# Gated delta attention with experts: k weighted ahead of the scan, z laid out by tokens, a mask by select, no product by the identity, and new task orders

## The chip, the cores and the metric

The kernel runs on one core of a Trainium2 chip. The metric is the device time of one execution in microseconds, the median of several runs. The core has TensorE (matrix products), VectorE, ScalarE and GpSimd (elementwise work), SyncE (which only issues DMAs here), SBUF for tiles, and PSUM, into which TensorE writes and which GpSimd does not read in this kernel. Each engine works through its own list of instructions in order; the engines meet only through semaphores.

## The reference

A layer with modulated layer norm, gated delta rule attention, a second layer norm and a mixture of six small experts (two per sample), for 8 samples of 512 tokens with 256 features. The part that the change touches is the attention: 16 key heads of 128, each with 2 value heads of 128. Cut to what matters:

```python
q, k, v = silu(conv4(h @ W_qkv.T))          # causal convolution over time, 4 taps
z = h @ W_z.T
q, k = l2norm(q) * dk ** -0.5, l2norm(k)
g = cumsum(g, within a chunk)
decay = where(tril, exp(g[:, None] - g[None, :]), 0)
A = -where(strict_tril, (beta * k) @ k.T * decay, 0)
T = inverse(eye - A)
value_, k_cumdecay = T @ (beta * v), T @ (beta * k * exp(g))
for each chunk:
    v_new = value_ - k_cumdecay @ state
    out = (q * exp(g)) @ state + where(tril, q @ k.T * decay, 0) @ v_new
    state = state * exp(g_last) + (k * exp(g_last - g)).T @ v_new
core = out * rsqrt(mean(out * out) + 1e-6)
y = (norm_weight * core * silu(z)) @ W_out.T
```

## The kernel before

`build` writes three stages. `modulation_and_gates` makes the first layer norm and all gate values and leaves them in DRAM. `attention` runs 128 steps, one for each pair of sample and key head. `experts` does the second norm, the choice of experts and their products. The change is in `attention`, but for one constant.

A step is cut into some 60 small tasks per engine, and the orders are written out as lists: `PE_ORDER`, `ACT_ORDER`, `DVE_ORDER`, `POOL_ORDER` (lines 34 to 44). An entry such as `M2@3` means: task M, part 2, of the step that is 3 ahead of this round's number. `loop` (line 510) walks the list once per round, two rounds in the body of a hardware loop, so that up to five steps are in flight and every engine repeats one list with the period of a step. Nothing moves an entry at run time: if one waits, all behind it on that engine wait. `t.wait(engine, name, k, back=b)` waits for the k-th signal of `name` of the step b before; `wait_newest` waits for the latest earlier user of a PSUM bank.

A step takes 4 chunks of 128 tokens (`NC`) and 2 value heads (`HD`), so 8 units (`U`). Its tasks, with what they hand on:

- TensorE P0 to P11 (line 658): the projection; tiles 0 to 3 are k, q and two of v, tiles 4 and 5 are z, all with channels on the partitions. ScalarE C and VectorE T0 to T11 (line 1018, three per tile) make the convolution, ScalarE SK, SQ, SV the silu, ScalarE Z (line 891) the silu of z into `z_t`.
- TensorE KT, QT, VT (lines 668 to 707): transposes to tokens; ScalarE KN, QN squares and VectorE KN, QN sums; GpSimd PW (line 1199) a power 0.5; VectorE SM0 to SM3 and SN0 to SN2 small scalings (lines 1034 to 1060; SN0 makes `w_c`, the factors of the state's update).
- GpSimd GL (line 1194): `low = g_row + bound`, where the constant `bound` is 0 or -1e30; ScalarE GE (line 924): eight exponentials of it into `dec`, behind a table load, since exponential and silu lie in different tables. TensorE KK0, KK1 (line 690): products of k by k and q. VectorE GA0 to GA3 (line 1072): `ga`, A and the attention weights. GpSimd SL (line 1203) sets the diagonal of A.
- The inverse of a 128 by 128 triangle: VectorE AB0, AB1 (line 1078) copy its two halves of 64 into `a_bd`; TensorE L, M1 to M5, Y1 to Y5 (lines 713 to 725), VectorE y0 to y5, q1 to q5, X1 to X5 (lines 1085 to 1102) and XB1 to XB5 on ScalarE (upper half, line 936) and GpSimd (lower half, line 1225) invert them level by level in bf16; Q, p, Z, XD, YC, XC join them; D0, D1, VectorE F0, F1 (line 1118), GpSimd RL (line 1217), G0, G1, ScalarE v0, v1 (line 970) and W0, W1 refine the result. W (line 793) adds, in PSUM, the old inverse by a product with the identity, and three more products; ScalarE IV0, IV1 (line 966) copy the sum into `inv_t`.
- The scan over chunks: TensorE KS, VectorE RR, TensorE TR; then VectorE VW (line 1140) makes `vw`, v_new times `w_c`, and ScalarE VX copies v_new into `vx`; TensorE U (line 826) is the product of `k_tok` and `vw`, VectorE ST adds it to the state, which GpSimd SD has decayed; TensorE O the output, ScalarE OT a copy.
- The output: ScalarE OQ sums of squares, VectorE OS0, OS1 (lines 1156, 1159), GpSimd OP (lines 1244, 1247: a power -0.5 and a product) and ON (line 1253: the scaling of `o_tok`); TensorE ON transposes it, VectorE HT (line 1164) multiplies by the norm weight and `z_t`, TensorE OY0, OY1 (line 868) the product by W_out, VectorE YA0, YA1 add it up.

KT, QT, VT, KK, D, G, W, ON and OY share the two PSUM banks `p_out`. SyncE feeds each step's weights and gate rows one to four steps ahead.

## Time and profile before

| | |
|---|---|
| median of three runs (lowest, highest) | 4832.42 us (4830.36, 4836.11) |
| span of the profiled execution | 4831.3 us |
| busy share of the span: TensorE, VectorE, ScalarE, GpSimd | 97%, 91%, 72%, 57% |
| mean granted TensorE clock | 0.987 |
| DMA | 377 MB, 78 GB/s, 24.7% of the engines' time |

The profile holds one execution. An instruction's duration reaches from its start to its end, and on TensorE the ends are modelled; consecutive instructions overlap, so what a task takes of its engine is better read as the distance from its start to the next start. "Idle before" is time in which the engine stood still ahead of an instruction, with the one that ended the wait. A product of float32 tiles is recorded as two matmul instructions.

### The profile page before, as it was taken

What the parts mean: (1) busy time and instruction counts of PE and PEld (TensorE: products, weight loads), DVE (VectorE), ACT (ScalarE), POOL (GpSimd) and SP (SyncE); (2) the same over time, 40 slices, a digit from 0 to 9 for tenths busy, and PEclk for the clock granted to TensorE, in tenths of its full rate; (3) what the DMA queues carried; (4) which work ended last, traced back from release to release, by engine and by line L of the source; (5) the groups of instructions that cost most, each with busy time, mean ns of one, the idle gap of its engine ahead of it and who ended that gap; (6) DMA issues with size and microseconds to landing.
All of it is one profiled execution on the core that took longest, in us unless ns stands there. A gap on an engine that the chain in (4) does not pass through costs nothing. (4 is left out here: it accounts for less than half of the span.)

```text
span 4831.3 us, 132942 instructions
## 1 busy us (share of the span) xinstructions
PE 4671.0 (97%) x38533; PEld 3195.1 (66%) x38788; DVE 4411.5 (91%) x9152; ACT 3467.6 (72%) x8336; POOL 2743.0 (57%) x2329
## 2 busy tenths in 40 slices
PE   5899999999999999999999999999999999999978
PEld 3566666666666666666666666666666666666643
DVE  4899999999999999999999999999999999999953
ACT  3677777777777777777777777777777777777732
POOL 2456665656565665656566665656566665656520
PEclk7999999999999999999999999999999999999988
DMA  4222222222222222222222222222222222222122
GB/s 156 65 75 79 68 86 70 88 66 87 67 79 79 68 86 71 88 66 87 67 80 79 68 86 66 92 66 84 70 78 80 66 87 66 92 66 84 55 79 83
DMA packets 185165, 377.26 MB, mean 78 GB/s; under 512 B 86400, under 2 KB 95744, under 8 KB 184960
## 3 DMA queue, kind: packets, MB, share of 16 engines
q1 hardware_dynamic: 185088, 376.46, 24.7%
q14 instruction: 57, 0.47, 0.0%
q8 instruction: 20, 0.33, 0.0%
HBM read 360.13 MB, written 16.25 MB: 78 GB/s over the span
## 5 line engine op out<-in xcount | busy, mean ns | idle before, releaser
L658 PE MATMUL p_proj<-hid,w_in 128*128 128x512 f32 x3072 | 1626.7, 612 | 30.0 <-POOL ident_h L1185 28.9
L1018 DVE SCALAR_TENSOR_TENSOR conv<-p_proj,taps,conv 128x509 f32<-128x509 f32 (+2 forms) x1536 | 1134.8, 739 | 48.2 <-ACT conv L886 34.9
L1199 POOL TENSOR_TENSOR root<-sums,half_pow 128x8 f32<-128x8 f32 x128 | 210.8, 1647 | 862.9 <-DVE sums L1028 843.9
L1225 POOL TENSOR_SCALAR_AFFINE_SELECT x_bd<-x_t 128x512 bf16<-128x512 bf16 x640 | 422.6, 660 | 213.5 <-DVE x_t L1102 211.2
L658 PEld LDWEIGHTS p_proj<-hid,w_in 128*128 128x128 f32 x3072 | 497.3, 192 | 55.1 <-POOL ident_h L1185 29.1
L1093 DVE TENSOR_TENSOR y_h<-p_lev,y_h 128x512 bf16<-128x512 f32 x640 | 440.2, 688 | 74.4 <-PE p_lev L725 74.4
L868 PE MATMUL p_out<-h_t,w_out 128*128 128x512 f32 x1024 | 476.5, 608 | 2.2 <-DVE h_t L1164 1.1
L936 ACT ACTIVATE x_bd<-x_t 64x512 bf16<-64x512 bf16 x640 | 397.7, 621 | 96.3 <-DVE x_t L1102 96.2
L1102 DVE STREAM_TRANSPOSE x_t<-y_h 128x512 bf16<-128x512 bf16 x640 | 450.3, 704 | 4.5
L1072 DVE SCALAR_TENSOR_TENSOR ga<-p_out,neg_c,dec 128x256 f32<-128x256 f32 x1024 | 412.9, 477 | 35.4 <-ACT dec L924 34.8
L886 ACT ACTIVATE conv<-p_proj,taps 128x512 f32<-128x512 f32 x512 | 351.7, 687 | 121.9 <-PE p_proj L658 119.3
L1085 DVE TENSOR_TENSOR q_h<-p_lev,consts 128x512 bf16<-128x512 f32 x640 | 429.6, 671 | 3.8 <-PE p_lev L718 3.8
L979 ACT ACTIVATE vx<-p_b 128x256 f32<-128x256 f32 x512 | 197.9, 386 | 285.8 <-PE p_b L816 161.4
L1217 POOL TENSOR_TENSOR r_lo<-resid 128x1024 bf16<-128x1024 f32 x128 | 242.3, 1893 | 247.9 <-DVE resid L1118 247.9
L838 PE MATMUL p_b<-vx,ga 128*128 128x128 f32 x2048 | 375.1, 275 | 0.0
L868 PEld LDWEIGHTS p_out<-h_t,w_out 128*128 128x128 f32 x1024 | 184.6, 190 | 285.0 <-DVE ga L1072 147.9
L725 PEld LDWEIGHTS p_lev<-q_h,x_bd 128*128 128x128 bf16 x5120 | 216.5, 97 | 213.5 <-issue 101.5
L985 ACT ACTIVATE o_tok<-p_b 128x256 f32<-128x256 f32 x512 | 194.1, 379 | 199.5 <-PE p_b L838 196.4
L718 PEld LDWEIGHTS p_lev<-y_h,a_bd 128*128 128x128 bf16 x5120 | 222.7, 98 | 152.1 <-issue 84.2
L1232 POOL TENSOR_TENSOR q_dec<-kq,e_row 128x512 f32<-128x512 f32 x256 | 320.0, 1271 | 0.0
L924 ACT ACTIVATE dec<-low,g_neg 128x128 f32<-128x128 f32 x1024 | 313.3, 388 | 1.6
L1244 POOL TENSOR_TENSOR o_sc<-o_sc,neg_half 128x8 f32<-128x8 f32 x128 | 211.4, 1651 | 168.9 <-DVE o_sc L1159 168.9
(213 smaller groups left out, 12562.4 us busy)
## 6 DMA issues: line engine op xcount, KB each, us to landing
w_in<-in_w_in SPq DMA_DIRECT2D x128, 768.0 KB, 6.3
g_row<-rows_scratch SPq DMA_DIRECT2D x128, 512.0 KB, 3.2
hid<-h_scratch SPq DMA_DIRECT2D x128, 512.0 KB, 7.4
e_row<-exp_rows_scratch SPq DMA_DIRECT2D x128, 512.0 KB, 5.3
w_out<-in_w_out SPq DMA_DIRECT2D x128, 256.5 KB, 2.7
x<-in_x SPq DMA_DIRECT2D x8, 512.0 KB, 10.6
...
```

The lines of the kernel that those rows point to most:

```text
L658: last = pe.matmul(p_proj[tile % 2][:], w_in[p][:, kt, tile * P:(tile + 1) * P], hid[p][:, kt, :], start=(kt == 0), stop=(kt == KT - 1))
L838: last = pe.matmul(p_b[:, at], ga[p][:, n * HD + h, 1, :], vx[:, h, :], start=(n == 0), stop=True)
L868: last = pe.matmul(p_out[n][:], w_out[p][:, h * D + n * P:h * D + (n + 1) * P], h_t[:, :, h, :], start=(h == 0), stop=(h == HD - 1))
L886: act.activation(conv[:, n, :], p_proj[n % 2][:], ACT.Copy, scale=taps[p][:, n, PAD:PAD + 1])\
L936: act.activation(x_bd[0:HB, :, 0:HB], x_t[0:HB], ACT.Copy).then_inc(s["xbd"], 1)
L1018: dve.scalar_tensor_tensor(conv[:, tile, late:], p_proj[tile % 2][:, 0:S - late], taps[p][:, tile, j:j + 1], conv[:, tile, late:], ALU.mul ...
L1072: last = dve.scalar_tensor_tensor(ga[p][:, u], kk, neg_c[p][:, n, h:h + 1], each(dec[:, u, :], 2), ALU.mult, ALU.mult)
L1085: dve.tensor_tensor(q_h[:], levels(), each(const["mask"][:, n * HB:(n + 1) * HB], U), ALU.mult)\
L1093: dve.tensor_tensor(y_h[:], levels(), y_h[:], ALU.add).then_inc(s["y_done"], 1)
L1102: dve.transpose(x_t[:].rearrange("p u f -> p (u f)"), y_h[:].rearrange("p u f -> p (u f)"))\
L1225: pool.affine_select(x_bd[:, :, HB:P], x_t[:], [[0, U], [0, HB]], ALU.is_ge, zero, base=-HB, channel_multiplier=1).then_inc(s["xbd_low"], 1)
L1232: last = pool.tensor_tensor(q_dec[p][:, :, h, :], kq[p][:, :, 1, :], e_row[p][:].rearrange("p (c h) i -> p c h i", h=HD)[:, :, h, :], ALU. ...
```

## The change

Six edits in the attention stage:

- `k_w` = `k_tok` times `w_c` is made for three chunks at once by GpSimd (KW); U is one product per value head of `k_w` and `vx`. VW and `vw` go away, and VX no longer waits for VW.
- z is projected with tokens on the partitions (hid is the stationary side), GpSimd's ON multiplies `o_tok` by it, in a second product, and HT, now on ScalarE, only scales the transposed tile by the norm weight.
- GL is an `affine_select` of `g_row` with -1e30 in place of the sum with `bound`.
- W has no product by the identity; IV, now on VectorE, adds `x_dn` as it reads PSUM.
- p is now ScalarE's PH.
- All four orders are new, and the `wait_newest` lists follow the new order of the banks' users.

```diff
-PE_ORDER = ("M2@3 ON1@1 O0@2 VT0@3 Y2@3 KS1@2 W1@2 M3@3 TR1@2 P0@4 Y3@3 U1@2 P1@4 M4@3 KS2@2 O1@2 P2@4 Y4@3 TR2@2 "
-            "P3@4 M5@3 VT1@3 O2@2 U2@2 P4@4 KS3@2 Y5@3 P5@4 KT@4 QT@4 XD@3 Q6@3 TR3@2 P6@4 Z6@3 P7@4 D0@3 O3@2 XC@3 "
-            "D1@3 KK0@4 KK1@4 P8@4 OY0@1 OY1@1 G0@3 L@4 P9@4 W0@3 M1@4 P10@4 TR0@3 Y1@4 G1@3 P11@4 U0@3 ON0@2")
-ACT_ORDER = ("GE@2 OT3@0 C3@2 OQ3@0 XC@1 SV0@2 AO@2 v0@1 IV0@1 XB1@2 VX0@1 v1@1 SV1@2 XB2@2 OT0@1 Z0@2 Z1@2 XB3@2 "
-             "IV1@1 VK0@2 VX1@1 C0@3 XB4@2 OT1@1 OQ0@1 VX2@1 C1@3 OQ1@1 XB5@2 OT2@1 VK1@2 OQ2@1 SK@3 SQ@3 C2@3 KN@3 "
-             "QN@3 XD@2 VX3@1 KT@3 YC@2")
-DVE_ORDER = ("T10@3 y0@3 T11@3 X1@3 q1@3 YA1@0 VW0@2 y1@3 X2@3 ST0@2 HT0@1 q2@3 HT1@1 y2@3 RR1@2 X3@3 q3@3 VW1@2 "
-             "y3@3 ST1@2 X4@3 q4@3 T0@4 RR2@2 T1@4 y4@3 VW2@2 X5@3 T2@4 q5@3 T3@4 ST2@2 T4@4 T5@4 y5@3 SN1@3 s11@3 "
-             "s10@3 RR3@2 T6@4 p6@3 KN@4 QN@4 T7@4 T8@4 SN2@3 F0@3 SM0@4 SM1@4 SM2@4 SM3@4 F1@3 SN0@3 GA0@4 GA1@4 "
-             "GA2@4 GA3@4 T9@4 YA0@1 OS0@2 AB0@4 AB1@4 OS1@2")
-POOL_ORDER = ("SL@3 OP@1 XB1@3 ON@1 XB2@3 SD1@2 GL@4 XB3@3 QD@3 XB4@3 AR@3 SD2@2 AL@3 XB5@3 PW@4 RL@3")
+PE_ORDER = ("P11@2 U0@1 O0@1 VT0@2 Y1@2 KS1@1 P0@3 M2@2 W1@1 P1@3 Y2@2 TR1@1 P2@3 U1@1 M3@2 O1@1 KS2@1 Y3@2 P3@3 TR2@1 ON0@0 "
+            "ON1@0 M4@2 U2@1 O2@1 Y4@2 VT1@2 KS3@1 P4@3 M5@2 P5@3 QT@3 Y5@2 KT@3 P6@3 Q6@2 XD@2 TR3@1 P7@3 Z6@2 O3@1 D0@2 XC@2 "
+            "D1@2 KK0@3 KK1@3 P8@3 OY0@0 OY1@0 G0@2 P9@3 W0@2 L@3 P10@3 TR0@2 M1@3 G1@2")
+ACT_ORDER = ("XB3@2 VK0@2 OT1@1 OQ0@1 C1@3 VX2@1 HT0@0 XB4@2 HT1@0 OT2@1 VK1@2 SK@3 SQ@3 XB5@2 C2@3 QN@3 KN@3 KT@3 PH@2 XD@2 "
+             "VX3@1 YC@2 OT3@1 OQ1@1 OQ2@1 C3@3 OQ3@1 XC@2 GE@4 v0@2 SV0@3 AO@3 VX0@2 XB1@3 SV1@3 v1@2 Z0@3 OT0@2 Z1@3 XB2@3 "
+             "C0@4 VX1@2")
+DVE_ORDER = ("IV1@1 y2@2 T0@3 X3@2 ST1@1 q3@2 T1@3 RR2@1 y3@2 T2@3 X4@2 T3@3 q4@2 ST2@1 T4@3 y4@2 T5@3 X5@2 q5@2 y5@2 s11@2 "
+             "SN2@2 s10@2 RR3@1 SN0@2 KN@3 T6@3 QN@3 T7@3 T8@3 F0@2 SM0@3 SM1@3 SM2@3 F1@2 SM3@3 GA0@3 GA1@3 GA2@3 OS0@1 GA3@3 "
+             "OS1@1 T9@3 YA0@0 AB0@3 T10@3 AB1@3 T11@3 YA1@0 IV0@2 y0@3 X1@3 q1@3 ST0@2 SN1@3 y1@3 X2@3 q2@3 RR1@2")
+POOL_ORDER = ("XB1@2 SD1@1 XB2@2 QD@1 XB3@2 AR@2 SD2@1 XB4@2 AL@2 GL@4 XB5@2 KW@2 PW@3 RL@2 SL@3 OP@1 ON@1")
...
-                    last = pe.matmul(p_proj[tile % 2][:], w_in[p][:, kt, tile * P:(tile + 1) * P], hid[p][:, kt, :],
-                                     start=(kt == 0), stop=(kt == KT - 1))
+                    if tile < 4:
+                        last = pe.matmul(p_proj[tile % 2][:], w_in[p][:, kt, tile * P:(tile + 1) * P], hid[p][:, kt, :],
+                                         start=(kt == 0), stop=(kt == KT - 1))
+                    else:
+                        c = n - 4 * KT
+                        for k in range(KT):
+                            last = pe.matmul(p_proj[tile % 2][:, kt * HD * DH:(kt + 1) * HD * DH],
+                                             hid[p][:, k, c * CH:(c + 1) * CH], w_in[p][:, k, 4 * P:6 * P],
+                                             start=(k == 0), stop=(k == KT - 1))
...
-                    pe.matmul(p_out[n][:], ident_h[:], quarter(x_dn, n).rearrange("p a i -> p (a i)"),
-                              start=True, stop=False)
...
-                    pe.matmul(p_a[:, HD * DH:2 * HD * DH], k_tok[p][:, n, :], vw[:].rearrange("p h f -> p (h f)"),
-                              start=True, stop=True).then_inc(s["u_mm"], 1)
+                    for h in range(HD):
+                        last = pe.matmul(p_a[:, (HD + h) * DH:(HD + h + 1) * DH], k_w[p][:, n, h, :], vx[:, h, :],
+                                         start=True, stop=True)
+                    last.then_inc(s["u_mm"], 1)
...
+                elif name == "PH":
+                    t.wait(act, "q6_mm")
+                    t.wait(act, "z6_mm", back=1)
+                    act.activation(p_h[HB:P], p_lev[HB:P, :].rearrange("p (u f) -> p u f", f=HB), ACT.Copy).then_inc(s["p6_done"], 1)
...
+                elif name == "HT":
+                    t.wait(act, "on_mm", n + 1)
+                    t.wait(act, "y_out", back=1)
+                    act.activation(cols(h_t, n), bank(n), ACT.Copy, scale=const["norm_w"]).then_inc(s["h_done"], 1)
...
+                elif name == "IV":
+                    t.wait(dve, "w_mm", n + 1)
+                    t.wait(dve, "x12")
+                    t.wait(dve, "tr_mm", back=2)
+                    dve.tensor_tensor(quarter(inv_t[p], n), bank(n), quarter(x_dn, n), ALU.add).then_inc(s["inv_done"], 1)
...
-                    pool.tensor_tensor(low[:], g_row[p][:], each(const["bound"], U), ALU.add).then_inc(s["g_low"], 1)
+                    pool.sem_inc(passed, 1)
+                    pool.affine_select(low[:], g_row[p][:], [[0, U], [1, CH]], ALU.is_ge, far_below, base=0,
+                                       channel_multiplier=-1).then_inc(s["g_low"], 1)
...
+                elif name == "KW":
+                    t.wait(pool, "k_tok_done")
+                    t.wait(pool, "w_scaled")
+                    t.wait(pool, "u_mm", back=2)
+                    pool.tensor_tensor(k_w[p][:], k_tok[p][:, 0:NC - 1].unsqueeze(2).to_broadcast([P, NC - 1, HD, DH]),
+                                       w_c[p][:, 0:NC - 1].unsqueeze(3).to_broadcast([P, NC - 1, HD, DH]), ALU.mult)\
+                        .then_inc(s["kw_done"], 1)
...
                     pool.tensor_tensor(o, o, scale, ALU.mult).then_inc(s["o_nrm"], 1)
+                    t.wait(pool, "o_nrm", 1)
+                    t.wait(pool, "z_done")
+                    pool.tensor_tensor(o, o, z_t[p][:].rearrange("p c h f -> p (c h) f"), ALU.mult).then_inc(s["o_nrm"], 1)
```

## Rows read from the trace of the kernel before

**Rows 1.** One step: length, busy PE, PEld, DVE, ACT, POOL (instructions), clock, DMA.
```profile
1999.57:2034.72 35.15, 34.80 (x298) 24.07 (x299) 33.43 (x71) 26.39 (x65) 21.25 (x18) 1.00 0.25 76
```
**Rows 2.** The copies into a_off, one per step, with first and last start.
```profile
L929 ACT ACTIVATE a_off<-ga x128: 629/630/632, 138.8 to 4594.4; 64x512 bf16<-64x512 f32 x128
```
**Rows 3.** TensorE's timeline: start us, duration us, instructions; same-line neighbours merged.
```profile
2000.75 1.10 PE L658 MATMUL p_proj<-hid,w_in 128*128 128x512 f32 x2
2001.91 0.22 PE L796 MATMUL p_out<-x_dn,r_lo 128*128 128x128 bf16 x1
...
2002.52 0.22 PE L798 MATMUL p_out<-g_t,resid 128*128 128x128 bf16 x1
...
2019.54 1.02 PE L658 MATMUL p_proj<-hid,w_in 128*128 128x512 f32 x2
2020.40 0.59 PE L803 MATMUL p_a<-state,kq 128*128 128x256 f32 x2
2020.83 0.40 PE L725 MATMUL p_lev<-q_h,x_bd 128*128 128x64 bf16 x8
2021.07 1.10 PE L658 MATMUL p_proj<-hid,w_in 128*128 128x512 f32 x2
2022.01 0.60 PE L668 MATMUL p_out<-consts,kq 128*128 128x128 f32 x4
2022.44 0.60 PE L676 MATMUL p_out<-consts,kq 128*128 128x128 f32 x4
```
**Rows 4.** TensorE's timeline at KK0 and KK1 of the same step.
```profile
2028.76 1.08 PE L690 MATMUL p_out<-kq 128*128 128x256 f32 x4
2030.05 1.10 PE L690 MATMUL p_out<-kq 128*128 128x256 f32 x4 [0.21 <-DVE resid L1118]
```
**Rows 5.** VectorE's timeline at the same place: SM0 and F1.
```profile
2028.29 0.16 DVE L1034 TENSOR_SCALAR neg_n<-root 128x8 f32<-128x8 f32 x1
...
2029.22 0.69 DVE L1118 TENSOR_TENSOR resid<-p_out,consts 128x512 f32<-128x512 f32 x1
```
**Rows 6.** Groups by line on VectorE in that step: count | busy us, mean ns | idle before.
```profile
L1164 DVE SCALAR_TENSOR_TENSOR h_t<-p_out,norm_w,z_t 128x512 f32<-128x512 f32 x2 | 1.5, 746 | 0.1
L1118 DVE TENSOR_TENSOR resid<-p_out,consts 128x512 f32<-128x512 f32 x2 | 1.4, 688 | 0.0
...
L1140 DVE TENSOR_TENSOR vw<-p_b,w_c 128x256 f32<-128x256 f32 x3 | 1.2, 416 | 0.1
...
L1113 DVE CAST p_h<-p_lev 64x512 bf16<-64x512 f32 x1 | 0.7, 694 | 0.0
```
**Rows 7.** The same view, ScalarE.
```profile
L886 ACT ACTIVATE conv<-p_proj,taps 128x512 f32<-128x512 f32 x4 | 2.7, 686 | 0.6 <-PE p_proj L658 0.6
...
L924 ACT ACTIVATE dec<-low,g_neg 128x128 f32<-128x128 f32 x8 | 2.4, 387 | 0.0
```
**Rows 8.** The same view, GpSimd.
```profile
L1194 POOL TENSOR_TENSOR low<-g_row,consts 128x1024 f32<-128x1024 f32 x1 | 2.4, 2362 | 0.0
L1253 POOL TENSOR_TENSOR o_tok<-o_tok,o_sc 128x1024 f32<-128x1024 f32 x1 | 1.9, 1897 | 0.0
```
**Rows 9.** OS0 over the run (ns min/median/max); its longest beside SL.
```profile
L1156 DVE TENSOR_TENSOR o_sc<-o_ss,q_s x128: 156/161/712, 207.4 to 4647.3; 128x8 f32<-128x8 f32 x128
...
207.40 0.71 DVE L1156 TENSOR_TENSOR o_sc<-o_ss,q_s 128x8 f32<-128x8 f32 x1
...
207.00 1.10 POOL L1203 TENSOR_SCALAR_AFFINE_SELECT ga<-ga 128x1024 f32<-128x1024 f32 x1 [1.81 <-DVE ga L1072]
```
**Rows 10.** Timelines of GpSimd and VectorE: PW's power, and SN2 during it.
```profile
2026.36 1.65 POOL L1199 TENSOR_TENSOR root<-sums,half_pow 128x8 f32<-128x8 f32 x1 [6.69 <-DVE sums L1028]
...
2027.62 0.16 DVE L1060 TENSOR_SCALAR q_s<-inv 128x4 f32<-128x4 f32 x1
```
**Rows 11.** ScalarE's timeline in the first stage: a table load and its instruction.
```profile
76.67 1.28 ACT L305 ACT_TABLE_LOAD   x1
85.53 0.38 ACT L305 ACTIVATE gates<-p_ln 128x256 f32<-128x256 f32 x1 [7.58 <-DVE gtail L384]
```

More of the change, by code:

```diff
@@ L426, in attention @@
         k_tok, v_tok = two("k_tok", [P, NC, DH]), two("v_tok", [P, NC, HD, DH])
+        k_w = two("k_w", [P, NC - 1, HD, DH])
         eye_h, ident_h = sb("eye_h", [P, HB], BF), sb("ident_h", [P, P], BF)
@@ L913, in emit @@
                     t.wait(act, "kt_mm")
-                    t.wait(act, "u_mm", back=2)
+                    t.wait(act, "kw_done", back=2)
                     act.activation(k_tok[p][:], bank(0), ACT.Copy).then_inc(s["k_tok_done"], 1)
@@ L939, in emit @@
                     t.wait(act, "w_mm", back=1)
+                    t.wait(act, "inv_done", back=1)
                     act.activation(x_dn[:].rearrange("p u i -> p (u i)"), p_tr_h, ACT.Copy).then_inc(s["xdn"], 1)
@@ L1051, in emit @@
                         t.wait(dve, "scaled")
+                        t.wait(dve, "kw_done", back=2)
                         dve.tensor_tensor(w_c[p][:], neg_c[p][:], w, ALU.mult).then_inc(s["w_scaled"], 1)
@@ L1132, in emit @@
                     last.then_inc(s["rr_done"], 1)
-                elif name == "VW":
-                    t.wait(dve, "tr_mm", n + 1)
-                    if n == 0:
-                        t.wait(dve, "w_scaled")
-                        t.wait(dve, "u_mm", back=1)
-                    else:
-                        t.wait(dve, "u_mm", n)
-                    dve.tensor_tensor(vw[:], p_b[:, 0:HD * DH].rearrange("p (h f) -> p h f", h=HD),
-                                      over(w_c[p][:, n, :], [P, HD, DH]), ALU.mult).then_inc(s["vw_done"], 1)
                 elif name == "ST":
@@ L1154, in emit @@
                     t.wait(dve, "q_scaled", 1)
-                    t.wait(dve, "o_nrm", back=1)
+                    t.wait(dve, "o_nrm", 1, back=1)
                     dve.tensor_tensor(o_sc[:], o_ss[:], over(q_s2[p][:], [P, NC, HD]), ALU.mult).then_inc(s["osm"], 1)
```

108 lines of the change are left out of this document (46 added, 62 removed).

## The prediction

> **What bounds the kernel now.** I read the busy times of one step of the middle first, then the starts on TensorE's timeline, then VectorE's. One step (one sample, one key head; 128 of them) is the distance between two copies into `a_off`: 4455.6 us over 127 steps, 35.08 us each [rows 2], so 92% of the span is these steps. In one of them TensorE shows 34.80 of 35.15 us busy, VectorE 33.43, ScalarE 26.39, GpSimd 21.25, at a granted clock of 1.00 [rows 1]. TensorE's durations overlap, so they say little; its starts say more. A float32 projection task of 512 columns takes 0.86 us from start to start, a 256-column one 0.43, a group of eight 64-column bf16 products 0.24, a transpose 0.11 (four in 0.43), a 128-column bf16 product 0.055 (W's twelfth starts 0.61 after its first) [rows 3]. Where such a bf16 group stands ahead, a float32 task takes 0.94: its first weights lie bare for 0.08. With the counts of the code a step holds 13,568 columns of float32 product (22.8 us at 0.86 per 512), 24 float32 transposes (2.6), 64 bf16 products of 128 columns (3.5), 14 groups of 64 columns (3.3) and the identity products (0.43): 32.6 us. About twelve bare loads add 1.0. So 33.6 us are TensorE's own and **about 1.45 us per step are waits for others**. The largest I find is at KK1: 1.29 us between KK0 and KK1 where 0.86 are work [rows 4]. F1 comes late there, since VectorE's four small SM steps, each waiting for the last, stand ahead of it: 0.93 us from SM0 to F1 [rows 5]. VectorE is idle for 1.7 us of the step. The two engines are both near full, in fixed orders, and each waits a little for the other.
>
> **TensorE's part.** W loses its product by the identity. In the trace that matmul has hardly a record, but the hole is there: P10 starts at 2000.75 and takes 0.94, and the next recorded product starts at 2001.91, 0.22 later [rows 3]. Two per step give 0.43 us. U becomes two products of 128 columns in place of one of 256: as many columns, two more weight loads; I take +0.01 each, 0.04 per step. The projection of z now has chunks of hid as weights and w_in as the moving side: again 2048 columns in each layout, but eight products with their loads in place of four. KS and KK show 256 float32 columns in 0.43 with a load for each [rows 3, 4], so I price it at nothing; its cover is that a load runs under the product ahead. If each of the extra loads lay bare (4 here and 3 in U, two passes each, 14 times 0.08) it would cost 1.1 per step; that is the far bound. Nothing in it could gain, since no column goes away. TensorE's own work is then 33.6 - 0.43 + 0.04 = 33.2 us.
>
> **VectorE's part.** It loses three VW (0.416), two HT (0.746) and p (0.694): 3.43 us. It gains two IV, an addition of PSUM and a bf16 tile as wide as F (0.688): 1.38. Net **-2.06 us** per step [rows 6], so its busy time falls to about 31.4, and it is no longer near the bound. The gain counts only where it lets TensorE wait less.
>
> **ScalarE and GpSimd.** ScalarE takes PH and two HT and gives up two IV, each a copy of 512 float32 columns, at most 0.69 [rows 7]: +0.7 of 35. GpSimd: GL becomes a select over 1024 elements, 1.10 as SL [rows 9] where the sum took 2.36; the new product by z lies between the 1.90 of the scaling and the 2.36 of the old GL, I take 2.4 as both its inputs are full tiles; KW multiplies 768 elements, so 1.4 to 1.8 by the same two rows [rows 8]. Net +2.7, to 24 of 35. KW waits for SN0 of its step, and k_w is wanted only at U0, in the next round of the lists. Queued behind KW on GpSimd are PW, RL, SL, OP. PW needs QN's sum; on VectorE SN0 is followed by KN, T6 and QN, each about as long as F's 0.69,, so KW, started after SN0, is done before the sum is there, and costs nothing. Without that cover it would put up to 1.8 us ahead of SM0 and so of KK1.
>
> **The order, around its tightest place.** Let a be the start of GA0. In both kernels it hangs on F1, KK0 and SM3. *Ahead of a:* D0, O3, XC, D1, KK0, KK1 becomes D0, XC, D1, KK0, KK1. F0, and behind it SM0 to SM2, start nearer to D1's end, and only SM3 moves behind F1; I keep KK1's wait of about 0.45. *Behind a, TensorE:* GA1 is done at a+1.7, then OY0 and OY1 (3.5 with a bare load), G0 0.2, P9 0.9: W0 at a+6.4. *ScalarE:* GE now stands for a step further ahead, directly ahead of v0, and waits for GA3 of the step before it (`back=1`), done at a+3.35. Queued behind GE are v0, SV0, AO, VX0. GE's eight exponentials take 2.45 (387 ns each, starts overlapping [rows 7]), v0 0.6: W0's input at a+6.45. Level. *GpSimd:* SL from a+3.5 to 4.6, OP to 6.6 (1.65 for a power [rows 10], a small product and latencies), the scaling to 8.5, the product by z to 11.0, and only then GpSimd's half of XB1 (0.7, estimated from SL's 1.10 at half the elements), to 11.7. TensorE, behind W0: 0.66, L, P10, TR0, M1, G1, P11, U0, O0, VT0, together 5.0: Y1 at a+11.5. So Y1 waits some 0.2. The old order had XB1 between OP and the scaling; **this chain is what is late next**. Elsewhere (VX1 to U1 to ST1 to KS2, X to Y, PH to Z6) I find the producer 0.1 to 0.5 us ahead of its user.
>
> **The sum.** Waits: 0.45 at KK1, 0.2 at Y1, 0.25 for the rest, where VectorE's 2 us of room should have done away with most of the old 1.0. 33.2 + 0.9 = 34.1 us per step, 0.97 less; times 128 is 124 us. What lies around the steps (4831.3 - 4455.6 = 375 us) is not touched, but for 64 KB less of constants. The profiled span 4831.3 becomes 4707, and the median of the runs shown lies 1.1 above the span: **4708 us**.
>
> **Rivals.** *Waits all but gone:* 0.25 are left; 33.45, 1.62 less a step, about **4625**. For it: VectorE's room. Against: KK1's wait rests on latencies that stay.
>
> *Only the product counts:* the waits stay at 1.4 since the orders are as tight as before; 0.39 saved, 50 us, **4782**. Bare loads of z and U (up to 1.1, 141 us) would bring the forecast to 4849 and this case to 4923; I give that end little.
>
> *The cast behind the power (slower):* GpSimd and VectorE hold each other up in this trace: OS0, an 8-element product with two inputs in SBUF, 0.16 in the median, took 0.71 once when SL was running, and ended 0.01 after it [rows 9]. In the new order OP follows SL at once (its input OS1 now comes ahead of SL's end, not behind AB1), so AB0 and AB1, which read SBUF, start under OP's power of 1.65 us. If that holds them up, AB0 ends at a+6.7 in place of 5.0, AB1 falls under the scaling and waits for its end, and L comes at a+9.4 where it wanted 7.1: 2.3 us per step on top of 34.1, about **5000**. It decides once casts are kept out for more than 1.1 us in all, since AB1 would else end at a+6.0. Against: SN2 starts under PW's power in the steps of before and still takes 0.16 [rows 10]; the other small VectorE steps and the casts into y_dn stand where GpSimd waits, and SN1, with two SBUF inputs, about where the product by z ends, ahead of a y1 that waits for Y1 anyway. The Trainium skill (SBUF — State Buffer, Who interferes with whom) makes it a lock held for the whole instruction, taken by VectorE copies and casts in a two-port mode and by its instructions with two SBUF inputs. By that rule, with which the OS0 row agrees, AB0 would be kept out; SN2 under PW shows nothing of it.
>
> *The table load behind the wait (slower):* GE needs a load of 1.28 us. If it ran only after GA3, v0 and W0 would be 1.3 late: 35.4, **4870**. Against: in the first stage the load ran at once and its instruction then waited 7.58 us [rows 11].
>
> **How the numbers follow.** Forecast (4670 to 4750) 0.54; waits all but gone 0.12; only the product 0.16; about unchanged 0.04; cast behind the power 0.09; table load or another chain of more than 1 us 0.05. Range: the first three, 4630 to 4810, leave out the slow cases and the tails. 0.2% (10 us) is about what a measurement of this kernel can tell from no change: faster 0.82, same 0.04, slower 0.14.
>
> **What would show it.** TensorE: no hole behind P10 or M2 ahead of W, U groups of 0.44, P8 to P11 still 0.86. KK0 to KK1 still near 1.3. VectorE's busy time per step near 31.4, with idle time ahead of y (waiting for Y) in place of work. ScalarE: a table load that starts before GA3 ends, `dec` right behind GA3, g_t right behind it. GpSimd: z's product of 2.4, XB1 right behind it, Y1 within 0.3 of XB1's need. a_bd casts of 0.42 though OP runs. The forecast is wrong if the casts grow past 1 us, if TensorE idles ahead of W0, L or Y1 by more than 0.5, or if the new z products take over 0.95 a task.

## The result and the profile after

The changed kernel takes 4803.7 us (median; 4802.7 to 4810.7) beside 4832.1 for the kernel before on the same chip: ratio 0.994, 95% interval 0.9927 to 0.9952. It is faster, but by 28 us where 124 were forecast (4708). The time lies inside the stated range (4630 to 4810), at its slow end. The profiled execution spans 4802.5 us.

The page's busy shares answer to the table of before: VectorE fell from 91% to 87%, GpSimd rose from 57% to 64%, TensorE stayed at 97%.

```profile
PE 4646.8 (97%) x40324; PEld 3411.7 (71%) x40324; DVE 4174.1 (87%) x8640; ACT 3587.4 (75%) x8462; POOL 3078.2 (64%) x2585
```

Two neighbouring steps (columns as in [rows 1]; steps alternate between two lengths, the two rounds in the loop's body):

```profile
1958.23:1993.27 35.04, 34.78 (x312) 25.79 (x310) 31.59 (x68) 27.40 (x66) 23.95 (x21) 1.00 0.25 76
1993.27:2027.91 34.64, 34.47 (x312) 25.76 (x310) 31.59 (x67) 27.30 (x67) 23.78 (x21) 1.00 0.25 77
```

The copies into `a_off`, as in [rows 2], give the mean step:

```profile
L934 ACT ACTIVATE a_off<-ga x128: 612/613/619, 142.3 to 4568.5; 64x512 bf16<-64x512 f32 x128
```

(4568.5 - 142.3) / 127 = 34.85 us per step, 0.23 less than 35.08. VectorE's busy time is 31.59 (forecast 31.4), GpSimd's 24 (forecast 24): both sizes were right. What did not come is time. TensorE's timeline of the changed kernel: KK0, KK1, P8, OY0 and OY1, then P9 and W0's first product:

```profile
2018.39 1.10 PE L697 MATMUL p_out<-kq 128*128 128x256 f32 x4
2019.66 1.10 PE L697 MATMUL p_out<-kq 128*128 128x256 f32 x4 [0.17 <-DVE resid L1125]
2020.60 1.03 PE L664 MATMUL p_proj<-w_in,hid 128*128 128x256 f32 x4
2021.50 3.70 PE L873 MATMUL p_out<-h_t,w_out 128*128 128x512 f32 x8
...
2025.26 1.08 PE L664 MATMUL p_proj<-w_in,hid 128*128 128x256 f32 x4
2026.20 0.22 PE L802 MATMUL p_out<-x_dn,r_lo 128*128 128x128 bf16 x1
```

P9 starts at 2025.26 and W0's first product 0.94 later: the hole of 0.22 that the identity product left [rows 3] is gone. (In both lists the projection task right ahead of W0 is P9; the prediction calls it P10, and means the same rows.) KK0 to KK1 are 1.27 apart, as 1.29 in [rows 4]. From P8 to OY0 are 0.90 with z by tokens, 0.04 of them a wait ahead of OY0.

To see where a step's time lies I took, over 100 steps of each trace, the distance from each TensorE start to the next and subtracted the smallest one of its kind. Before: 32.56 us of columns (with 0.43 for the identity products, which have no records), 1.90 in holes under 0.115 us (bare loads of 0.08 and short hand-overs) and 0.61 in larger ones. After: 32.18, 1.98 and 0.66. So 0.38 did leave TensorE's columns, 0.1 came back in small holes, the large waits did not shrink at all, and all together are 0.25 us per step. Of the small holes some ten per step before and eight after are 0.08 long, the bare loads (0.82 and 0.67 us), and 0.3 us are differences of a few ns; of the rest, about 0.8 before and 1.0 after, the starts do not tell how much is TensorE's own and how much short waits.

VectorE's timeline from F0 on, in the same step (columns: start, duration, instruction, idle before):

```profile
2017.55 0.69 DVE L1125 TENSOR_TENSOR resid<-p_out,consts 128x512 f32<-128x512 f32 x1 [0.18 <-PE p_out L774]
...
2018.82 0.69 DVE L1125 TENSOR_TENSOR resid<-p_out,consts 128x512 f32<-128x512 f32 x1
2019.43 0.16 DVE L1056 SCALAR_TENSOR_TENSOR neg_c<-cc,inv 128x8 f32<-128x8 f32 x1
2019.78 2.45 DVE L1083 SCALAR_TENSOR_TENSOR ga<-p_out,neg_c,dec 128x256 f32<-128x256 f32 x6 [0.20 <-DVE neg_c L1056]
...
2024.39 0.42 DVE L1089 CAST a_bd<-ga 64x512 bf16<-64x512 f32 x1
...
2026.62 0.74 DVE L1167 SCALAR_TENSOR_TENSOR y_acc<-y_acc,w_out,p_out 128x512 f32<-128x512 f32 x1
2027.28 0.68 DVE L1130 TENSOR_TENSOR inv_t<-p_out,x_dn 128x512 f32<-128x512 f32 x1
...
2030.79 0.42 DVE L1150 COPY state<-p_a 128x256 f32<-128x256 f32 x1 [0.91 <-PE p_a L833]
...
2031.91 0.69 DVE L1104 TENSOR_TENSOR y_h<-p_lev,y_h 128x512 bf16<-128x512 f32 x1 [0.52 <-PE p_lev L733]
```

This is the view to learn from. VectorE is idle for 3.45 us of the step, but from F0 (2017.55) to IV0's end (2027.96) it has hardly a pause. IV0 gates TR0, which starts at 2028.06, 0.1 behind it. The 2 us that VectorE was relieved of turned into idle time elsewhere (ahead of ST0, ahead of y1), where TensorE is the one it waits for. GpSimd's timeline over the same stretch (SL, OP's power, the product by z, XB1):

```profile
2023.26 1.10 POOL L1202 TENSOR_SCALAR_AFFINE_SELECT ga<-ga 128x1024 f32<-128x1024 f32 x1 [1.77 <-DVE ga L1083]
2024.32 1.65 POOL L1250 TENSOR_TENSOR o_sc<-o_sc,neg_half 128x8 f32<-128x8 f32 x1
...
2028.39 2.37 POOL L1262 TENSOR_TENSOR o_tok<-o_tok,z_t 128x1024 f32<-128x1024 f32 x1
2030.71 0.67 POOL L1224 TENSOR_SCALAR_AFFINE_SELECT x_bd<-x_t 128x512 bf16<-128x512 bf16 x1
```

And TensorE's TR0, VT0 and Y1:

```profile
2028.06 0.68 PE L822 MATMUL p_b<-v_tok,inv_t 128*128 128x128 f32 x4
...
2031.04 0.60 PE L714 MATMUL p_out<-consts,v_t 128*128 128x128 f32 x4
2031.48 0.39 PE L733 MATMUL p_lev<-q_h,x_bd 128*128 128x64 bf16 x8
```

XB1 ends at 2031.38 and Y1 starts at 2031.48, just when VT0's four transposes (0.44) are through as well: GpSimd and TensorE arrive at Y1 together in this step. In every second step Y1 waits 0.15, 0.08 in the mean. (VectorE's q1 had ended at 2029.88 and ScalarE's half of XB1 at 2029.97.) In the kernel before, the profile names ScalarE at another such place, GA0: this is GA's row in the whole run of before, by line (count | busy us, mean ns | idle before and what ended it):

```profile
L1072 DVE SCALAR_TENSOR_TENSOR ga<-p_out,neg_c,dec 128x256 f32<-128x256 f32 x1024 | 412.9, 477 | 35.4 <-ACT dec L924 34.8 <-PE p_out L690 0.6
```

and the same of the changed kernel:

```profile
L1083 DVE SCALAR_TENSOR_TENSOR ga<-p_out,neg_c,dec 128x256 f32<-128x256 f32 x1024 | 422.6, 477 | 25.0 <-DVE neg_c L1056 24.6
```

Before, the last thing that the profile names ahead of GA0 is ScalarE's `dec` (34.8 us over 128 steps), which the prediction had not seen. After, it is SM3's `neg_c`. But the starts say that neither moved GA0 by much: it stands 1.40 us behind KK0's start before and 1.44 after (means of 100 steps), and between 1.40 and 1.44 in thirteen of the variants below, with 1.40 in `b_three`, where `dec` comes early. KK0's product sets GA0; `dec` and `neg_c` come level with it.

### The profile page after: what moved, and what is told of

The parts are those of the page before. It is cut to its first block and busy times, and to the rows that moved or that the text cites. A ratio compares the mean times of both kernels' runs of the same rounds, so it can differ in the third digit from the quotient of the medians.

```text
span 4802.5 us, 136256 instructions
## 1 busy us (share of the span) xinstructions
PE 4646.8 (97%) x40324; PEld 3411.7 (71%) x40324; DVE 4174.1 (87%) x8640; ACT 3587.4 (75%) x8462; POOL 3078.2 (64%) x2585
## 5 line engine op out<-in xcount | busy, mean ns | idle before, releaser
L659 PE MATMUL p_proj<-hid,w_in 128*128 128x512 f32 x2048 | 1078.9, 609 | 29.6 <-POOL ident_h L1182 28.9
L664 PE MATMUL p_proj<-w_in,hid 128*128 128x256 f32 x2048 | 555.4, 394 | 0.9 <-DVE conv L1028 0.9
L1083 DVE SCALAR_TENSOR_TENSOR ga<-p_out,neg_c,dec 128x256 f32<-128x256 f32 x1024 | 422.6, 477 | 25.0 <-DVE neg_c L1056 24.6
L1238 POOL TENSOR_TENSOR k_w<-k_tok,w_c 128x768 f32<-128x768 f32 x128 | 188.3, 1471 | 355.0 <-DVE w_c L1063 346.0
L664 PEld LDWEIGHTS p_proj<-w_in,hid 128*128 128x128 f32 x2048 | 361.0, 191 | 42.5 <-DVE conv L1028 1.4
L659 PEld LDWEIGHTS p_proj<-hid,w_in 128*128 128x128 f32 x2048 | 331.4, 192 | 47.7 <-POOL ident_h L1182 29.2
L843 PE MATMUL p_b<-state,q_dec 128*128 128x128 f32 x1536 | 317.6, 288 | 0.6 <-ACT vx L985 0.5
L1004 ACT ACTIVATE o_junk<-o_tok 128x128 f32<-128x128 f32 x1024 | 304.6, 301 | 11.9
```

The source lines that it names most:

```text
L659: last = pe.matmul(p_proj[tile % 2][:], w_in[p][:, kt, tile * P:(tile + 1) * P], hid[p][:, kt, :], start=(kt == 0), stop=(kt == KT - 1))
L664: last = pe.matmul(p_proj[tile % 2][:, kt * HD * DH:(kt + 1) * HD * DH], hid[p][:, k, c * CH:(c + 1) * CH], w_in[p][:, k, 4 * P:6 * P], st ...
L1083: last = dve.scalar_tensor_tensor(ga[p][:, u], kk, neg_c[p][:, n, h:h + 1], each(dec[:, u, :], 2), ALU.mult, ALU.mult)
```

## The experiments

Each ran in five rounds beside the kernel before; the four of a group ran on one chip. A ratio is to the kernel before, with its 95% interval. Between two kernels I take the difference of ratios times 4835 us; each ratio is uncertain by about 0.0013, 6 us, and a difference of two of them by up to 9. Where I name a wait in a run's trace per step, it is read from TensorE's starts as above.

### Undo or do one part: the identity product, columns of VectorE, the order at KK

`b_noident` (the sum in W then lacks `x_dn`), from the kernel before:

```diff
-                    pe.matmul(p_out[n][:], ident_h[:], quarter(x_dn, n)..., start=True, stop=False)
```

> The kernel before, with one part of the change alone: W has no product by the identity (so the old inverse is missing from inv_t, and the output differs); the orders and all else stay. Theory A: of the 35.08 us of a step nearly all that is not TensorE's streaming is TensorE's own (bare weight loads, small gaps between groups), and the waits for others are under 1 us, so TensorE's work comes off one for one: 2 x 0.216 us a step, 55 us, some 4777 us. The whole change then loses 27 us again elsewhere. Theory B, as in my prediction: 1.45 us a step are waits of engines that are level; VectorE takes over as the bound when TensorE gets shorter, and less than half comes off: under 27 us, above 4805 us.

4833.3 us, ratio 0.9996 (0.9987 to 1.0005). Removing the product from the kernel before gains nothing. Theory A fell. Theory B's bound (above 4805) holds, but the prediction's own sum, which took the product in full, fell with it.

The trace shows where the 0.43 went. The wait at KK is the same (0.29 and 0.29), and new holes stand ahead of Y1 (0.15 more), TR1 (0.13), Y3 (0.07) and G1 (0.03), 0.4 with some smaller ones. At TR1 it is VectorE that is late. Its timeline from HT1 on (HT1, y2, RR1), then TensorE's M3 and TR1:

```profile
2010.53 0.74 DVE L1162 SCALAR_TENSOR_TENSOR h_t<-p_out,norm_w,z_t 128x512 f32<-128x512 f32 x1
2011.19 0.69 DVE L1091 TENSOR_TENSOR y_h<-p_lev,y_h 128x512 bf16<-128x512 f32 x1
2011.96 0.61 DVE L1127 SCALAR_TENSOR_TENSOR rr<-p_a,g_exp,v_tok 128x128 f32<-128x128 f32 x2
```
```profile
2012.17 0.40 PE L718 MATMUL p_lev<-y_h,a_bd 128*128 128x64 bf16 x8
2012.63 0.71 PE L814 MATMUL p_b<-rr,inv_t 128*128 128x128 f32 x4
```

M3 is through after 0.24, and TR1 starts 0.22 later, 0.06 behind RR1's end; RR1 stands in a stretch of VectorE without a pause. HT1 is one of the tasks that the change takes off VectorE, so the two edits can be of use to each other; that this very pair makes the difference is read from the trace, not tested.

`b_vec` and `a_vec`, VectorE's T on half its columns, from the kernel before and from the changed one (the rest of the convolution's sum is left out):

```diff
-   dve.scalar_tensor_tensor(conv[:, tile, late:], p_proj[tile % 2][:, 0:S - late], ...
+   dve.scalar_tensor_tensor(conv[:, tile, late:late + 256], p_proj[tile % 2][:, 0:256], ...
```

> The kernel before, with VectorE's twelve taps T on 256 of their 509 to 511 columns (the convolution of the other columns lacks three taps, so the output differs). VectorE loses about 12 x 0.27 = 3.2 us a step, more than the 2.06 that the change takes from it. Theory A (waits for VectorE are few, the rest is TensorE's own): at most 0.4 us a step, 50 us off, 4782 us or more. Theory B (my prediction: VectorE's room does away with about 0.8 us of waits a step): 100 us or more off, 4732 us or less.

> The changed kernel, with the same shorter taps: VectorE loses another 3.2 us a step (the output differs, since three taps are missing from the other columns). Theory A: TensorE waits at KK0 and KK1 only for F0, SM0 to SM2 and F1, which hang on D0, D1 and PW and not on VectorE's load, so less than 0.15 us a step, 20 us, 4784 us or more. Theory B: VectorE's load still sets the waits, 50 us or more off.

`b_vec` 4825.8 us, ratio 0.998 (0.9971 to 0.9989); `a_vec` 4795.1, ratio 0.9917 (0.9903 to 0.993). Some 2.5 us of VectorE's busy time per step (2.6 and 2.4) are worth 10 us of the run before and 11 after, so in both theory A holds and theory B, the prediction's, falls. In `b_vec` (whole run, by line) TensorE's idle time at KK is gone but for short waits (15.9 us before):

```profile
L690 PE MATMUL p_out<-kq 128*128 128x256 f32 x1024 | 273.9, 395 | 0.2 <-DVE resid L1118 0.2
```

and GA0's wait for `dec` on VectorE has grown from 34.8 to 56.1 us:

```profile
L1072 DVE SCALAR_TENSOR_TENSOR ga<-p_out,neg_c,dec 128x256 f32<-128x256 f32 x1024 | 412.9, 476 | 56.9 <-ACT dec L924 56.1 <-PE p_out L690 0.8
```

By the starts, KK1's wait falls from 0.29 to 0.12 us per step, and the one ahead of OY0, which needs GA, grows from 0.12 to 0.28. So the wait that the prediction called the largest can shrink by more than half, and time hardly moves, since the same chain claims it one task later.

`v_both`, the changed kernel with two edits of order:

```diff
-D1@2 KK0@3 KK1@3 P8@3 OY0@0          (TensorE)
+D1@2 KK0@3 P8@3 KK1@3 OY0@0
-SM2@3 F1@2 SM3@3 GA0@3               (VectorE)
+SM2@3 SM3@3 F1@2 GA0@3
```

> The changed kernel with two entries moved: on TensorE P8 stands between KK0 and KK1, on VectorE SM3 ahead of F1, so that GA0 finds neg_c ready and KK1 finds F1 done. The computation is the same. Theory A (the place D0, F0, SM, F1, KK1, GA0, OY0 is where the change lost 0.25 us a step): OY0 starts 0.2 us earlier and 25 to 30 us come off, about 4775 us. Theory B (the place only hides another wait of the same size right behind it, as in GpSimd's chain SL, OP, ON, XB1, Y1): within 10 us of the changed kernel.

4804.1 us, ratio 0.9936 (0.9923 to 0.995), no gain, as theory B said. KK1 (2021.50 here) no longer waits; the wait stands ahead of OY0 instead, on TensorE's timeline:

```profile
2021.50 1.03 PE L697 MATMUL p_out<-kq 128*128 128x256 f32 x4
2022.81 1.55 PE L873 MATMUL p_out<-h_t,w_out 128*128 128x512 f32 x3 [0.28 <-DVE ga L1083]
```

### The same product in the changed kernel, both reliefs before, GA0 earlier, z as before

`a_ident`: the product put back, IV a plain copy.

```diff
+                    pe.matmul(p_out[n][:], ident_h[:], quarter(x_dn, n)..., start=True, stop=False)
-                    dve.tensor_tensor(quarter(inv_t[p], n), bank(n), quarter(x_dn, n), ALU.add)
+                    dve.tensor_copy(quarter(inv_t[p], n), bank(n))
```

> The changed kernel with the identity product put back (TensorE adds x_dn in PSUM again, the step IV on VectorE is a plain copy); everything else as changed, and the same is computed. In the kernel before, taking this product away alone saved nothing (ratio 0.9996, 0.9987 to 1.0005). Theory 'several chains end together': before, TensorE's own work and the chain over VectorE to KK1 and GA0 (with the ScalarE chain to GE beside it) are within some tenths of a microsecond per step of each other, so relief of one alone gains nothing; in the changed kernel VectorE's and ScalarE's chains have been shortened and TensorE's own work decides. Then two products of 0.216 us per step cost in full: 128 x 0.43 = 55 us over the changed kernel (4804), so about 4858, at least 4840. Rival 'the product runs in TensorE's waits': it costs nothing here either, since what is late are waits around KK1; then within 15 us of the changed kernel, 4804 to 4819.

4837.1 us, ratio 1.0002 (0.9993 to 1.0011): 30 us over the changed kernel, between the two theories. It also says what the rest of the change is worth without this edit: nothing. And the product is worth nothing without the rest (`b_noident`). Only together do they give the 28 us.

`b_noident_vec` is both edits of the first group on the kernel before.

> The kernel before with both reliefs that gained nothing or little each: without the identity product (4833.3) and with the step T of VectorE on 256 of its columns (4825.8). It leaves out half of T's update, so its output is another. Theory 'three chains end together': TensorE is relieved by 0.43 us and VectorE by over 1 us per step, but the chain over ScalarE, YC to GE with its table load of 1.28 and the exponential of 2.45 to GA0, stays where it is: 4810 to 4833. Rival 'two chains': with both relieved the gain is at least the smaller relief, 128 x 0.43 = 55 us: 4780 or less.

4798.0 us, ratio 0.9923 (0.9909 to 0.9937): 37 us, where the two alone gave 2 and 10. Both theories missed the number; that together they gain more than the sum of the two is clear.

`v_sm`, the changed kernel with P8 between KK0 and KK1 and

```diff
-KN@3 T6@3 QN@3 T7@3 T8@3 F0@2 SM0@3 SM1@3 SM2@3 F1@2 SM3@3 GA0@3
+KN@3 QN@3 T6@3 T7@3 T8@3 SM0@3 F0@2 SM1@3 SM2@3 SM3@3 F1@2 GA0@3
```

> The changed kernel with P8 between KK0 and KK1 on TensorE and, on VectorE, the order KN QN T6 T7 T8 SM0 F0 SM1 SM2 SM3 F1 GA0; the same is computed. With P8 alone between them (v_both) nothing was gained: 0.38 us of TensorE's wait moved from KK1 to OY0, which needs GA0's gate, and GA0 started at the same time, at the end of F0, SM0 to SM3, F1. Here QN comes ahead of T6, so GpSimd's power of the sums can start some 0.4 us earlier, and the small steps of SM0 run before F0 instead of behind it. Theory 'VectorE's chain from F0 to GA0 is what is late': GA0 starts 0.3 to 0.4 us earlier and OY0's wait of 0.48 falls by as much, 128 x 0.35 = 45 us: about 4760 against the changed kernel's 4804. Rival 'what is late next is as late': the time that GA0 gains is lost to the next wait (T6 frees its PSUM tile 0.4 us later, D1 or the projections wait for it), and the run is within 10 us of 4804.

4808.9 us, ratio 0.9947 (0.9933 to 0.9961), no gain. SM3 and F1 are early now, and GA0, on VectorE's timeline, waits for KK0 itself:

```profile
2022.65 2.05 DVE L1083 SCALAR_TENSOR_TENSOR ga<-p_out,neg_c,dec 128x256 f32<-128x256 f32 x5 [0.30 <-PE p_out L697]
```

GA0 starts 1.40 us behind KK0's start here, and 1.39 in the changed kernel, where SM3 was named. The two releasers were level, and neither of the two orders moved GA0; F0, KK0, GA0 is a chain: KK0 starts 0.15 behind F0's end in all three kernels.

`a_zold`, z projected as before (its columns then lie wrongly for the later steps):

```diff
-                    if tile < 4:
+                    if tile < 6:
```

> The changed kernel with z's tiles projected in the old layout, four products of 512 columns instead of sixteen of 128 (same columns in sum, a quarter of the weight loads, and the output is another since the halves no longer lie as the later steps expect). Theory 'as priced': loads of 128 columns are hidden behind products of 128 columns, so z by tokens costs TensorE nothing and the run is within 10 us of the changed kernel (4804). Rival 'bare loads': a load is uncovered at each of up to eight changes of weight; the far bound of the prediction was 1.1 us per step of both halves, and the run gains up to 80 us, 4725 to 4790.

4804.8 us, ratio 0.994 (0.9926 to 0.9953): z by tokens costs TensorE nothing that these runs can show, as priced.

### How much of a cut in TensorE comes through, and GpSimd's product

`a_w2` leaves out W's second product:

```diff
-                        pe.matmul(bank(n)[:, u - n * 4, :], top(resid[:, u, :]), x_dn[:, u, :], start=False, stop=False)
```

and `a_w1` the first as well:

```diff
-                        pe.matmul(bank(n)[:, u - n * 4, :], r_lo[:, u, :], x_dn[:, u, :], start=True, stop=False)
```

> The changed kernel with the second of W's three products left out (eight bf16 products of 128 columns, 8 x 0.055 = 0.44 us of TensorE per step; the output is another). It is the counterpart to the identity product: the same size, the same place, taken away instead of put back. Putting 0.43 back cost 0.24 us per step (4837 against 4804). Theory 'TensorE decides in the changed kernel': the 0.44 is gained in full or nearly, 128 x 0.44 = 56 us, so 4748, at most 4765. Rival 'another chain is level with TensorE at 34.8 us per step', as it was in the kernel before, where the same cut gained nothing: within 15 us of 4804.

> The changed kernel with two of W's three products left out (0.88 us of TensorE per step; the output is another). Theory 'TensorE decides': the first 0.44 in full, the second in full or in part as other chains come level, 4690 to 4730. Rival 'another chain level at 34.8': within 15 us of 4804, and as a_w2. The two together give the slope: gain for the first and for the second 0.44 us.

`a_w2` 4778.8 us, ratio 0.9885 (0.987 to 0.99); `a_w1` 4773.0, 0.9872 (0.9857 to 0.9887). The first 0.44 us (56 us of TensorE) gives 27, between what the two theories said, and the second 6; for both together the theory had 4690 to 4730. The trace says why the first gives half. In `a_w2`, TensorE's P10 and TR0:

```profile
2013.46 1.11 PE L664 MATMUL p_proj<-w_in,hid 128*128 128x256 f32 x4
2014.64 0.68 PE L821 MATMUL p_b<-v_tok,inv_t 128*128 128x128 f32 x4
```

and VectorE's IV0 ahead of it:

```profile
2013.86 0.68 DVE L1129 TENSOR_TENSOR inv_t<-p_out,x_dn 128x512 f32<-128x512 f32 x1
```

P10 to TR0 is 1.18 us where 0.96 were before the cut (2027.10 to 2028.06): TensorE comes 0.22 earlier and waits 0.2 for IV0, whose place VectorE's unbroken stretch sets. That is W0's half of the cut. W1's half lies behind Y1 and comes through: 128 x 0.22 = 28.

`a_nozmul` takes GpSimd's product by z away (one on 8 elements stands in its place, so the output lacks z):

```diff
-   pool.tensor_tensor(o, o, z_t[p][:].rearrange("p c h f -> p (c h) f"), ALU.mult)
+   pool.tensor_tensor(spare[:], neg_half[:], neg_half[:], ALU.mult)
```

> The changed kernel without GpSimd's product of o_tok by z_t, 2.37 us of GpSimd per step (the output is another). In the trace that product is followed by GpSimd's half of XB1, which ends 0.1 us ahead of Y1's start. Theory 'just in time': Y1 waits 0.08 us per step at most, so the gain is within 10 us: 4794 to 4804. Rival 'this chain, or what VectorE loses beside it (SN1 takes 0.21 to 0.41 us in place of 0.15), is what is level with TensorE': a gain of 20 us or more.

4794.4 us, ratio 0.9915 (0.9901 to 0.9928): 12 us for 2.37 us of GpSimd per step. The theory "just in time" (10 at most) holds within the uncertainty: Y1's wait of 0.08 per step, 10 us of the run, is gone in this trace, and no other changes by 0.01.

`b_three` is `b_noident_vec` with one exponential in place of GE's eight:

```diff
-                    for u in range(U):
-                        last = act.activation(dec[:, u, :], low[:, u, :], ACT.Exp, bias=g_neg[p][:, u:u + 1])
+                    last = act.activation(dec[:], low[:], ACT.Exp)
```

> The kernel before without the identity product, with VectorE's step T on 256 of its columns, and with ScalarE's GE as one exponential over 1024 elements without a bias in place of eight (about 1.1 us in place of 2.45; the output is another). Without the third edit it takes 4798 (ratio 0.9923), where 'three chains' expected 4810 or more and 'two chains' 4780 or less: both missed. If the ScalarE chain YC, table load, GE, GA0 is what holds it at 34.80 us per step, this run gains at least 30 us more: 4770 or less. If it is TensorE's own work with the latencies around KK, as in the changed kernel (34.83), it gains at most 10: 4788 to 4798.

4791.6 us, ratio 0.9912 (0.9898 to 0.9925), 5 us more, which is no more than the uncertainty: ScalarE's chain is not what holds it. GA0's idle time stayed (54.9 us, from 56.9) and changed its releaser, from `dec` to KK0's product:

```profile
L1069 DVE SCALAR_TENSOR_TENSOR ga<-p_out,neg_c,dec 128x256 f32<-128x256 f32 x1024 | 412.9, 476 | 54.9 <-PE p_out L690 54.8
```

### The head and the end of the stretch

`a_f` and `b_f`: F0 and F1 on two of their four units each (the residual of the others stays zero).

```diff
-   dve.tensor_tensor(quarter(resid, n), bank(n), each(const["ident"], 4), ALU.add)
+   dve.tensor_tensor(quarter(resid, n)[:, 0:2], bank(n)[:, 0:2], each(const["ident"], 2), ALU.add)
```

> The changed kernel with F0 and F1 on 256 of their 512 columns (about 0.42 us in place of 0.69 each; the residual of half the units stays zero, so the output is another). KK0 waits 0.14 us for F0 and KK1 0.38 for F1, and GA0 starts when both are through. Two changes of order (v_both, v_sm) could not move GA0. Theory 'the stretch from D1 over F, KK and GA0 to IV0 is a chain of its own that decides': KK0 and GA0 start earlier by 0.14 to 0.5 us, and all of it is gained: 128 x 0.4 = 51 us, about 4755 and at most 4775. Rival 'place, not cause': the wait turns up elsewhere, within 12 us of 4804.

> The kernel before with the same edit. The prediction named the wait at KK1 (0.4 us) as the largest. Theory 'in the kernel before too the stretch over F and KK to GA0 decides, and neither the product nor columns elsewhere on VectorE': 128 x 0.4 = 51 us, about 4785, at most 4805. Rival 'several chains level': at most 15 us, 4820 or more.

`a_f` 4784.9 us, ratio 0.9896 (0.9881 to 0.9911): 21 us, less than my theory's 29 at least and more than the rival's 12. `b_f` 4835.2, 0.9998 (0.9989 to 1.0007): nothing, as the rival said; KK1's wait (0.29) is gone in its trace, and 0.36 more stand ahead of OY0. In `a_f` TensorE's waits at KK (0.53 us per step) are gone, and OY0 waits 0.37 longer for GA:

```profile
2008.92 1.98 PE L697 MATMUL p_out<-kq 128*128 128x256 f32 x8
2010.74 1.03 PE L664 MATMUL p_proj<-w_in,hid 128*128 128x256 f32 x4
2012.01 1.98 PE L873 MATMUL p_out<-h_t,w_out 128*128 128x512 f32 x4 [0.25 <-DVE ga L1083]
```

The difference, 0.53 - 0.37 = 0.16 us, times 128 is the 21 us. In the changed kernel the wait at KK was partly a cause: cut it, and the next link of the same chain is there after a third of the way.

`a_w2_vec` is `a_w2` with T on 256 columns; `a_w2_iv` is `a_w2` with

```diff
-T11@3 YA1@0 IV0@2 y0@3
+T11@3 IV0@2 YA1@0 y0@3
```

> The changed kernel without W's second product (a_w2, 4779) and with VectorE's step T on 256 columns (a_vec, 4795; 9 us alone). The output is another. In a_w2 TR0 waits 0.20 us per step for IV0, at the end of a stretch of VectorE without a pause that holds T9, T10 and T11. Theory 'VectorE's stretch takes W0's half of the cut': TR0's wait of 0.20 falls away, 128 x 0.2 = 25 us more than a_w2, and a_vec's 9: 4745 to 4756. Rival 'the gains only add': 4779 - 9 = 4770, or more.

> As a_w2, but VectorE takes IV0 ahead of YA1 in place of behind it; nothing else differs. Theory 'VectorE's stretch': IV0 ends 0.66 us earlier, TR0's wait of 0.20 falls away, and the run takes 4779 - 25 = 4754, unless G1, which needs YA1 on the same bank, takes it back. Rival 'TR0's wait is a place, not the cause': within 8 us of 4779.

`a_w2_vec` 4766.9 us, ratio 0.9854 (0.9839 to 0.987): 15 us beyond `a_w2`. TensorE's TR0, VT0 and Y1:

```profile
2009.49 0.61 PE L821 MATMUL p_b<-v_tok,inv_t 128*128 128x128 f32 x4
...
2012.27 0.60 PE L714 MATMUL p_out<-consts,v_t 128*128 128x128 f32 x4
2013.15 0.39 PE L733 MATMUL p_lev<-q_h,x_bd 128*128 128x64 bf16 x8 [0.28 <-issue]
```

and GpSimd's XB1:

```profile
2012.37 0.68 POOL L1223 TENSOR_SCALAR_AFFINE_SELECT x_bd<-x_t 128x512 bf16<-128x512 bf16 x1
```

TR0's wait is gone, as expected, but VT0 to Y1 is 0.88 us where 0.44 are work: Y1 starts 0.10 behind the end of GpSimd's XB1 (2013.05). Nothing else is near: VectorE's q1 ends at 2011.12, ScalarE's half of XB1 at 2011.21. Relieve VectorE, and GpSimd's chain takes the gain. The rival's number (4770) was nearer, for a reason that it did not name.

`a_w2_iv` 4813.7 us, ratio 0.9952 (0.9939 to 0.9966): 32 us **slower** than `a_w2`; both expectations missed. IV0 is ready for TR0, but it has to wait for W0's products, and YA1, which could have run in that time, now stands behind it and ahead of y0, which M1 needs. VectorE stands still for 0.23 us ahead of IV0 (mean of 100 steps), where in `a_w2` its tasks there overlap by 0.08; that is the 0.3 that y0 is late. TensorE's TR0 and M1, then VectorE's IV0, YA1, y0:

```profile
2026.97 0.61 PE L821 MATMUL p_b<-v_tok,inv_t 128*128 128x128 f32 x4
2028.00 0.41 PE L726 MATMUL p_lev<-y_h,a_bd 128*128 128x64 bf16 x8 [0.42 <-DVE y_h L1100]
```
```profile
2025.99 0.69 DVE L1129 TENSOR_TENSOR inv_t<-p_out,x_dn 128x512 f32<-128x512 f32 x1
2026.60 0.74 DVE L1166 SCALAR_TENSOR_TENSOR y_acc<-y_acc,w_out,p_out 128x512 f32<-128x512 f32 x1
2027.26 0.68 DVE L1100 TENSOR_TENSOR y_h<-p_lev,consts 128x512 bf16<-128x512 f32 x1
```

M1 waits 0.63 us per step, three times what TR0 had. It confirms from the other side that VectorE's stretch is tight: a swap of two tasks of 0.7 us in it costs 32 us.

Of the variants that keep the whole computation (`v_both`, `v_sm`, `a_ident`), none beat the changed kernel. `a_w2_vec` without GpSimd's product by z would have shown what Y1's wait of 0.4 us there is worth; it was not tried.

## Why the prediction was wrong, and where it was right

**Right.** Each size: the identity's hole gone; VectorE at 31.59 (31.4); z's product 2.37 (2.4), KW 1.47 (1.4 to 1.8), the select 1.10; z by tokens at nothing (`a_zold`); KK0 to KK1 unchanged; and the table load of GE ran ahead of its wait, with `dec` right behind GA3 (its end is 2023.09) on ScalarE's timeline:

```profile
2020.29 1.28 ACT L929 ACT_TABLE_LOAD   x1
2023.12 2.45 ACT L929 ACTIVATE dec<-low,g_neg 128x128 f32<-128x128 f32 x8 [1.55 <-DVE ga L1083]
```

So the rival of the table load fell. The rival of the cast behind the power fell too: AB0 starts 0.07 us into OP's power (2024.39) and takes 0.42, as AB0 and AB1 do in all 256 cases. Right as well was the sentence that GpSimd's chain to XB1 "is what is late next": Y1 comes within 0.1 us of it, and it takes 0.4 us per step as soon as TensorE and VectorE leave room (`a_w2_vec`).

**The step that failed is the waits' term of the sum:** 0.9 us after the change, "where VectorE's 2 us of room should have done away with most of the old 1.0". The prediction took 0.4 us off TensorE's own work (33.6 to 33.2) and 0.55 off the waits (1.45 to 0.9). The first came: TensorE's columns went from 32.56 to 32.18. The second did not: of the step's 34.85 us, 33.2 leave 1.65 for waits and not 0.9. These 0.75 us, times 128, are the 96 us by which the forecast missed. The waits over 0.115 us alone, 0.61 before and 0.66 after, did not shrink either.

"1.45 us of waits" was a remainder, not a reading: of it only the 0.4 at KK1 had a row. Larger waits were 0.6 of it. The rest lay in holes too small to be named, and only some of them can be waits; with every small hole counted as its own, TensorE had 34.5 of 35.08 us, and 34.2 of 34.85 after the change. So there was less to win than the sum supposed.

**Behind that is a wrong model.** The prediction let VectorE's 2 us of room do "away with most" of the waits, and let the identity's 0.43 come off in full. The runs show that both are conditional: the product alone gave 2 us, VectorE's columns alone 10, F alone 1, product and columns together 37. Before, TensorE's own work is level with VectorE's tasks in several places: at KK1 (behind F1), at OY0 (behind GA), at Y1 and at TR1 (behind RR1). What is taken from one place stands again at the next (`b_noident`, `b_vec`, `b_f`). The change relieves both engines, so it gains 28, and with the product put back nothing of that is left (`a_ident`, 30 us slower). After the change, TensorE, VectorE and GpSimd are level within about 0.1 to 0.4 us along the stretch from D1 over F, KK and GA to TR0 and Y1. VectorE's relief (VW, HT, p) fell outside this stretch, while IV0's 0.68 and the product by z were put into it.

**The line "in both kernels GA0 hangs on F1, KK0 and SM3" missed `dec`.** The row above, by line over the whole run, would have shown it: nearly all of GA0's idle time before ended with ScalarE. It cost the forecast little. KK0, which the line does name, sets GA0, and with `dec` short (`b_three`) KK0's product took its place for a gain of 5 us. What the line left unsaid is the length: 1.40 us from KK0 to GA0 that no edit of F, SM or `dec` shortened.

The rival "only the product counts" (4782) came nearest: it kept the waits, as the chip did, and erred by taking the product in full. It is this rival that stretches the range to 4810; the forecast's own band (4670 to 4750) and its mechanism do not reach the 4803.7, so that the time falls into the range is no merit of the forecast. In `a_w2`, of a cut of the same size at the same place, W1's half was gained and W0's was not. For `a_ident`, and so for the product itself, where the 0.19 us of the 0.43 that cost nothing go is only read from the trace (small waits at Y1, at P11 and around TR0 shrink by that much), not tested.

What stays open: how much of the 1.9 us of small holes an order could close, and which pair of edits it is that makes the product count in the changed kernel.
